# Gated cross-attention on one core: the last two tiles of 128 rows in another order

## The reference

```
n  = layernorm(x)
a  = softmax(n @ C^T) @ C                       # per batch, softmax over 77
x1 = x + tanh(g_xattn) * a
W' = W + up_aux @ (lora_up @ (lora_down @ down_aux))
y  = x1 + tanh(g_ffn) * (layernorm(x1) @ W'^T + b)
```

## Time and profile before

| | |
|---|---|
| runs, median | 319.59 us (319.36 to 319.92, three runs) |
| the profiled execution | 316.71 us |
| its span, first to last instruction | 314.9 us |
| mean granted TensorE clock | 0.995 |
| TensorE matmuls busy | 299.9 us (95%) |
| VectorE busy | 234.6 us (75%) |
| GpSimd busy | 221.3 us (70%) |
| ScalarE busy | 187.0 us (59%) |
| HBM | 167 GB/s over the span |
| time from one tile to the next, near the end | 4.32 us |

### The profile page before, as it was taken

One profiled execution on the slowest core, in us unless ns is written; L12 is line 12 of the kernel. 1 busy time (PEld: TensorE's weight loads), 2 busy tenths in 40 slices (PEclk: granted clock), 3 DMA queues, 4 the chain that ended last, 5 costly groups with the idle time before them and its releaser, 6 DMA issues.

```text
span 314.9 us, 6478 instructions
## 1 busy us (share of the span) xinstructions
PE 299.9 (95%) x2072; PEld 283.3 (90%) x2072; DVE 234.6 (75%) x745; ACT 187.0 (59%) x546; POOL 221.3 (70%) x271
## 2 busy tenths in 40 slices
PE   4788999999999999999999999999999999999991
PEld 0668999998999999999899999999899999999981
DVE  3685778797588877798497778788587778777864
ACT  1674665656476565666466566656476665656651
POOL 3136777777577778777577877778488777887752
PEclk9999999999999999999999999999999999999998
DMA  7947254455398655555199765555198955443112
GB/s 218 412 184 192 91 191 166 176 202 203 126 262 263 221 193 200 200 202 203 65 260 288 233 223 200 202 185 180 39 285 282 275 203 201 166 177 127 67 46 89
DMA packets 17755, 60.60 MB, mean 192 GB/s; under 512 B 2360, under 2 KB 2360, under 8 KB 17722
## 3 DMA queue, kind: packets, MB, share of 16 engines
q1 hardware_dynamic: 17074, 59.26, 55.8%
q10 hardware_dynamic: 648, 0.95, 0.9%
HBM read 35.84 MB, written 16.78 MB: 167 GB/s over the span
## 4 chain that ended last, share of the span: by engine, by line
PE 90%; DMA 3%; ACT 1%; DVE 1%; SPq 1%; POOL 1%; issue 1%; POOLq 0%; DVEq 0%; ACTq 0%
PE y_ps L481 64%; PE y_ps L509 9%; PE a_ps L504 9%; PE c_ps L471 3%; DMA w_rows<-in_w 2%; PE y_ps L489 2%; DMA stacks<-v_lo 1%; SPq L220 1%; PE a_ps L471 1%; PE y_ps L539 1%; PE y_ps L548 1%; DVE o_sb L654 0%; ACT w_cent L412 0%; DVE x L616 0%; POOL x_bias L292 0%
## 5 line engine op out<-in xcount | busy, mean ns | idle before, releaser
L481 PE MATMUL y_ps<-wc,xT 128*128 128x334 f32 (+1 forms) x1536 | 228.1, 302 | 0.0
L481 PEld LDWEIGHTS y_ps<-wc,xT 128*128 128x128 f32 x1536 | 214.3, 189 | 2.0
L292 POOL TENSOR_TENSOR x_bias<-x,bias_g 128x512 f32<-128x512 f32 x63 | 81.1, 1288 | 65.4 <-DVE x L616 65.4
L280 POOL TENSOR_TENSOR xT<-xt_raw,xT 128x512 fp32r<-128x512 f32 x64 | 83.3, 1301 | 9.5 <-ACT xT L357 9.5
L372 ACT ACTIVATE expd<-y_ps,neg_max,rs 128x77 f32<-128x77 f32 x64 | 26.6, 416 | 81.9 <-DVE neg_max L606 81.9
L386 ACT ACTIVATE squares<-x,x_nmean 128x512 f32<-128x512 f32 x64 | 46.4, 725 | 18.7 <-DVE x_nmean L624 18.7
L303 POOL TENSOR_TENSOR rs<-stat_eps,half_neg 128x2 f32<-128x2 f32 (+1 forms) x67 | 46.1, 688 | 5.2
L654 DVE SCALAR_TENSOR_TENSOR o_sb<-y_ps,rs,x_bias 128x512 f32<-128x512 f32 x64 | 48.0, 751 | 1.6 <-POOL rs L303 1.6
L509 PEld LDWEIGHTS y_ps<-stacks,pT 109*128 109x128 f32 (+1 forms) x256 | 39.8, 191 | 5.4
L637 DVE TENSOR_TENSOR pT<-y_ps,pT 13x128 fp32r<-13x128 f32 x64 | 18.6, 290 | 34.9 <-ACT pT L363 34.9
L616 DVE SCALAR_TENSOR_TENSOR x<-a_ps,x_sb 128x512 f32<-128x512 f32 x64 | 43.7, 683 | 1.2 <-PE a_ps L504 1.2
(11 more groups left out here) (64 smaller groups left out, 181.1 us busy)
## 6 DMA issues: line engine op xcount, KB each, us to landing
xt_raw<-in_xt SPq DMA_DIRECT2D x32, 512.0 KB, 6.0
x_sb<-in_x SPq DMA_DIRECT2D x32, 512.0 KB, 5.0
out<-o_sb SPq DMA_DIRECT2D x31, 512.0 KB, 3.3
stacks<-v_hi SPq DMA_DIRECT2D x8, 308.0 KB
stacks<-v_hi SPq DMA_DIRECT2D x8, 256.0 KB
stacks<-v_lo SPq DMA_DIRECT2D x8, 256.0 KB
w_rows<-in_w ACTq DMA_DIRECT2D x1, 512.0 KB, 4.7
w_rows<-in_w SPq DMA_DIRECT2D x1, 512.0 KB, 7.6
```

What stands on the lines that cost most here:

```text
L280: pool.tensor_tensor(xT[:, k % TRING, 1, :, :], xt_raw[:, k % XRING // UNIT, k % UNIT, :, :], xT[:, k % TRING, 0, :, :].bitcast(F32), ALU. ...
L292: pool.tensor_tensor(x1_bias[:, q, :], x1[:, j, :], bias_g[:, :], ALU.add).then_inc(x1b_ready, 1)
L481: mm = pe.matmul(y_half(k, h)[:, 0:n], xT[:, k % TRING, part, c, :], wc[:, c, w, h * H:h * H + n], start=(c == 0 and part == 0 and w == 0) ...
```

## The change

Only the last two tiles (62 and 63, T-2 and T-1) change.

- TensorE runs its ordinary steps up to 62, and leaves chunks 2 and 3 of half 0 of tile 62 out of step 62. A new function `last_two` then writes out the rest: half of tile 63's scores, transpose of 62, the other half of the scores, the chunks left out, p_product of 62, one chunk of half 0 of tile 63, transpose of 63, the other three chunks, p_product of 63.
- The two transposes go to `c_ps`, columns 0 to 127 and 128 to 255, with the flag that starts a new sum.
- ScalarE's variance of tile 62 moves behind p_hi of tile 63, and `squares` becomes two buffers.
- VectorE's output of tile 61 moves behind p_lo of tile 63, and the output of tile 62 behind x1, mean and biased x1 of tile 63.

The diff:

```diff
-        squares = sb("squares", [P, D])
+        squares = sb("squares", [P, 2, D])
...
         def p_transposed(k):
+            if k >= T - 2:
+                return c_ps[:, (k - T + 2) * P:(k - T + 3) * P]
             return y_half(k, 0)[:, H:H + P]
...
-        def all_tiles(step, prep):
+        def all_tiles(step, prep, until=T + 1):
 
-            for t in range(T + 1):
+            for t in range(until):
...
             def step(t, k):
                 if real(t - 1):
                     p_hi(t - 1, k - 1)
+                if t == T:
+                    variance(t - 2, k - 2)
...
-                if real(t - 1):
+                if real(t - 1) and t != T - 1:
                     variance(t - 1, k - 1)
...
-                          is_transpose=True, start=False, stop=True, skip_group_check=True).then_inc(pt_ready, 1)
+                          is_transpose=True, start=(t >= T - 2), stop=True, skip_group_check=True).then_inc(pt_ready, 1)
...
-                if real(t):
+                if real(t) and t != T - 2:
                     x_product(t, k, 0, range(KC // 2, KC))
+
+            def last_two():
+
+                a, b = T - 2, T - 1
+                pe.wait_ge(xl_ready, b + 1)
+                pe.wait_ge(out_ready, b - YRING + 1)
+                x_product(b, b, 1, range(0, KC // 2))
+                p_transpose(a, a)
+                x_product(b, b, 1, range(KC // 2, KC))
+                x_product(a, a, 0, range(KC // 2, KC))
+                p_product(a, a)
+                x_product(b, b, 0, range(0, 1))
+                p_transpose(b, b)
+                x_product(b, b, 0, range(1, KC))
+                p_product(b, b)
...
-            all_tiles(step, prep)
+            all_tiles(step, prep, T - 1)
+            last_two()
...
                 if real(t):
                     maxima(t, k)
-                if real(t - 2):
+                if real(t - 2) and t < T - 1:
                     output(t - 2, k - 2)
...
                 if real(t):
                     p_lo(t, k)
-                else:
+                if t >= T - 1:
+                    output(t - 2, k - 2)
+                if t == T:
                     output(t - 1, k - 1)
```

More of the change, by code:

```diff
@@ L385, in variance @@
                 act.wait_ge(nmean_ready, t + 1)
-                act.activation(squares[:, :], x1[:, k % 2, :], ACT.Square, bias=x1_nmean[:, k % 2:k % 2 + 1],
+                act.activation(squares[:, k % 2, :], x1[:, k % 2, :], ACT.Square, bias=x1_nmean[:, k % 2:k % 2 + 1],
                                scale=D ** -0.5, accum_out=stat[:, s, 2:3]).then_inc(var1_ready, 1)
```

## The result

| | before | after |
|---|---|---|
| median of 16 runs each | 319.39 us (317.20 to 319.92) | 316.88 us (315.52 to 317.99) |
| ratio, 95% interval | | 0.9926 (0.9904 to 0.9947) |
| the profiled execution | 316.71 us | 317.17 us |
| its span | 314.9 us | 315.4 us |
| a_ps of tile 61 to the start of the last output | 11.30 us | 9.76 us |

The changed kernel's median is 2.5 us lower, 0.7%, where 1.4 us was forecast (318.2 us, range 317.6 to 318.9). Two later comparisons gave ratios of 0.9930 (0.9902 to 0.9957) and 0.9945 (0.9927 to 0.9963), so the gain is more likely near 2 us than 2.5. Four of all the executions used here, with spans of 373 to 1657 us (three of the kernel before, one of a variant), lie far outside the rest and are left out of every ratio and every mean.

The account below looks back on a forecast made before the run. TensorE, busy 95% of the span, bounds the kernel; at the end one thin chain does. Gains 0.49 + 0.38 + 0.31 + 0.21 = 1.39 us, taken off the median 319.59, give 318.2 us, range 317.6 to 318.9.

Parts of the forecast that it names:

- Step 1: Scores of tile 63 ahead of six matmuls of tile 62: maximum of 63 earlier, held by p_lo of 62; gain 0.49 us.
- Step 2: Output of tile 61 out of the way of tile 63's inverse: counted as nothing, bound some tenth of a us.
- Step 3: Transpose of tile 63 after one chunk of half 0, a bare 0.47 us behind the probabilities: gain 0.38 us.
- Step 4: Variance of tile 62 behind p_hi of tile 63, so p_hi follows its transpose by a bare 0.35: gain 0.31 us.
- Step 5: p_lo, p_product, x1 of tile 63: x1 no longer held by output of 62, gain 0.21 us; output of 61 covered.
- Step 6: From x1 of tile 63 to the last output: 2.71 us, unchanged.
- step 7: Stores at the end: store of tiles 60 and 61 two us later, yet the stores don't meet; cost 0.
- step 8: TensorE's wait moved forward to about 301.2, inputs ready by 0.15; step 1 would hide 0.2 late; cost 0, bound 0.3.
- less than the sum: Rival: thin margins of steps 3, 5 and 8 turn into waits, gain 0.7 to 1.1, 318.7 us; chance 0.12.
- the stores didn't meet: Rival: slow earlier stores delay the last one, all gain gone, 319.6 us; chance 0.09 together with nothing gained.
- the clock didn't fall in the gaps: Rival: TensorE granted 1.2 GHz in one of the new gaps, some 323 us; chance 0.03.
- A second HAM failure mode: psum-queue depth-cycling: Rule bearing on steps 3 and 5: an engine idling briefly between groups of matmuls can swing between both clocks.

Follow-up runs that it names:

- the kernels with dummies: Nine or fifteen dummy matmuls in TensorE's set-up waits: kernel before 318.05 or 316.66 us, changed kernel 314.45 or 314.53 us.
- the delayed kernel: Changed kernel with seven dummy matmuls ahead of the last p_product, tail delayed to 11.40 us; ratio to before 0.9996 (0.9981 to 1.0012).

## Why the prediction was wrong

The place, the mechanism and the sign were right; the size wasn't, by 1.1 us against the first comparison. That parts in two: 0.15 us in the tail, and 1.0 outside it. The step that failed is the last one of the sum, from the profiled execution to the median of the runs ("so the same is taken off"), with 0.3 us for scatter and nothing for a difference outside the tail: with the tail's measured 1.54 the same sum would have given 318.05 us, still 1.2 over the 316.88 measured.

**The tail: 1.54 instead of 1.39.** By the steps:

- Step 1 forecast 0.49 and got 0.69. What failed is "that doesn't move" of p_lo of tile 62. I had p_hi of 62 behind the variance of 61, but it began 0.30 behind its transpose (302.77 against 302.47), the bare distance; the variance let go just before. The transpose now is 0.24 earlier, p_hi 0.12 (there the variance does hold it) and p_lo 0.14. The other 0.06 is that VectorE begins the next instruction before the row of the last has ended (305.48 against 305.27 + 0.28). That p_lo, not the scores, would hold the maximum was right, but only just. The forecast had the scores allow it 0.14 before p_lo. It counted the transpose of 62 twice, as 0.11 and again within the 0.27 (the rows at 302.47 and 302.49 start 0.02 apart). Without that the scores allow 3.10 in the table's terms, and the maximum began at 3.13.
- Step 2 forecast 0, bound some tenth, and got 0.07. With the output of 61 put back it is 0.10, of which TensorE hides all but 0.04.
- Step 3 forecast 0.38 and got 0.27. The transpose came 0.58 behind the probabilities, not 0.47: it was TensorE, not the hand-over, that ended the wait, since the probabilities were earlier than forecast and three matmuls still stood ahead. The absolute time (4.96 against 5.12) was better all the same. It is the 305.30 at which step 3 had TensorE arrive and wait for 0.16 (305.30 - 300.34 = 4.96): the arrival was right, the wait wasn't there.
- Step 4 forecast 0.31 and got 0.35 (the bare distance is 0.31 where the transpose didn't wait for the probabilities, and 0.35 where it did, as in tile 0); the variance put back costs more, 0.67, because in the new order p_hi is ready earlier and the variance isn't. The same edit has another price in either kernel: 0.35 is its term in the sum over the old chain, 0.67 what it would cost to leave it out.
- Step 5 forecast 0.21 and got 0.21 at x1; from p_hi to a_ps it was 1.01 instead of 0.99, with TensorE's nine matmuls just within (the 0.16 us of idling of the weight load; the forecast had 0.18). The output of 61 was covered as forecast. What I didn't price is what the output of 62 would have cost in its old place once the variance had moved: 1.29.
- Step 6 forecast no change of 2.71 and got 2.74. Steps 7 and 8 cost 0, as forecast. (In step 7 the bytes of before end 2.8 behind the output's start, 307.40 - 304.62, not 2.9.) The margin of step 8 was used up in the kernels with dummies, and step 1 didn't hide the delay.

0.69 + 0.07 + 0.27 + 0.35 - 0.02 + 0.21 - 0.03 = 1.54.

The first three terms aren't three gains. Before and after, TensorE works without an idle row from a_ps of 61 to the transpose of 63. In the new order nine matmuls of 256 columns fewer stand in between; at 0.117 each that is 1.05, and the transpose came 1.03 earlier, which is 0.69 + 0.07 + 0.27. The maximum and the probabilities only had to keep up, and did with 0.11 to spare (4.38 + 0.47 = 4.85 against 4.96).

**The rest: the sum was taken to the wrong base.** The prediction set the difference of 2.88 between the median and the profiled execution aside with "the end isn't where such a difference would sit". That is true, but it was the sign that single executions differ by more than the range's 0.3 to either side allowed. The three runs shown lay within 0.56 us; of all 16 the lowest was 317.20. The scatter has two parts, the set-up (most of it, by the traces, the clock there) and the time outside the span, and both go into the medians. Over all executions whose span was recorded (87 of before, 28 of the change) the means are 319.18 and 316.95 us, 2.23 apart (the parts below are rounded one by one):

| | before | after | difference |
|---|---|---|---|
| tail, by the traces | 11.30 | 9.76 | 1.54 |
| rest of the span, mean | 305.72 | 305.34 | 0.38 |
| outside the span, mean | 2.17 | 1.85 | 0.31 |

The 0.38 isn't constant: where both kernels were timed side by side the mean spans differed by 1.9 and by 1.6 us, the second of which leaves nothing for it. A rest of this size isn't the change's own either: beside the runs of before timed with each, the rest of the mean span was lower by 0.49 with TensorE kept busy to the end and by 0.24 with the idle stretch filled, two kernels with the order of before, and by 0.37 in the delayed kernel. These three have one more `memset` on VectorE at their start. The 0.31 comes from 21 of the 87 executions of before, which took 2.9 to 3.7 us outside the span instead of 1.8; of the changed kernel's 28 none did. No trace shows what lies there. It isn't TensorE's new order as such, since the delayed kernel has it in two of twelve, and neither filling the idle stretch nor keeping TensorE busy to the end removed it. **This part stays open**: 1.54 us is shown in the chain of instructions, some 0.7 is only in the means of whole executions, and part of that may be which set-ups the runs met. The other 0.3 of the first comparison's 2.5 us didn't come again in the two later ones. What the new places of `squares` and of the code do to the set-up, if anything, wasn't tried by itself.

Of the rivals, "less than the sum" was on the wrong side, the stores didn't meet, and the clock didn't fall in the gaps: the granted clock is 1.00 in the windows above, up to 314.4, and the matmuls of the last two tiles have the prices of before. What the Trainium skill's page TensorE: Matmul & The Clock Gate says under "A second HAM failure mode: psum-queue depth-cycling" didn't show here, and was hardly put to the test: the new order leaves TensorE one short gap near the end, 0.16 us of a weight load before the last a_ps, and it cost no clock; the 1.37 us of before cost none either. The clock did matter, in the set-up, where the same kernel has it at either level in different executions; the rows of before showed it at full in one execution, and I didn't ask whether every execution had that. The same page of the Trainium skill says, under "What's actually happening", that the moment of full clock varies from run to run for one kernel; the traces here agree, with twelve products in 3.3 to 5.4 us.

## What to carry to other kernels

Where an engine idles at the end of a pipeline, put its remaining work between the steps of the last chain, and on the other engines move everything that the chain doesn't need behind what it does: but price the moves together, since one moved result (the variance) can turn the cost of another's old place (the output) from 0.21 us into 1.29. Anchor the comparison of two traces at a point behind which only the change differs. And before a few tenths of a per cent are forecast, look at how far single executions spread and which stretch spreads: here the set-up moved by more than the change.

## What the runs showed of the hardware

- The same twelve matmuls of the set-up took 3.3 us in one execution and up to 5.4 in others, which I read as the moment at which TensorE's full clock came. Fifteen dummy matmuls in its waits took 2.4 us off the median of before (316.66 against 319.06; the ratio, 0.9938 with 0.9907 to 0.9969, makes it 2.0), though only half the executions profited.
- After 2.8 us of waiting in the set-up matmuls that had run at full clock were back at half (1.97 us for eight transposes, against 1.07 ahead of the wait). In the tail, 1.37 us of idling cost none of it.
- The PEclk column said 1.00 from 16 to 21 us in the trace of the change, where twelve products took 5.13 us. In the trace of before with nine dummies, where they took 5.40, it said 0.50.
- In 21 of 87 executions of the kernel before, and in none of 28 of the changed one, the time around the span was 2.9 to 3.7 us instead of 1.8, with spans no longer than the others'. No trace caught one, and the cause is open.
